# Local attention divides by its softmax sums behind the weighted sums of the values, not ahead of them

## What is computed

```python
x = x + local_block(group_norm(x))          # 4 groups of images, 8 strips of windows each
h = layer_norm(x) * g + b; h = roll(h, 3, 3)
h = windows of 7x7 pixels                    # 16 images * 64 windows, L = 49 tokens each
q, k, v = split(h @ qkv_w.T + qkv_b)         # 4 heads of 8 channels
scores = q @ k.T / sqrt(8) + bias
attn = exp(scores - max) / sum(exp(scores - max))   # softmax over the 49 keys
o = (attn @ v) @ out_w.T + out_b
y = gelu(layer_norm(o) @ mlp_w1.T + mlp_b1) @ mlp_w2.T + mlp_b2
```

## Time and profile before

| what | value |
|---|---|
| median of three executions | 3361.59 us |
| the profiled execution | 3363.74 us |
| its span, from first to last instruction | 3361.9 us |
| mean granted clock of TensorE in it | 0.951 of full speed |
| the local block's units, first subtraction to last product ahead of them | about 98 to 975 us of the span |
| PE, DVE, ACT, POOL busy, whole span | 88%, 74%, 65%, 18% |

### The profile page before, as it was taken

How to read it: one execution, slowest core, us unless ns; L and a number is a source line. 1 busy time by engine, 2 the same in 40 slices (tenths; PEclk the granted TensorE clock), 3 DMA queues, 4 the chain that set the end, 5 groups by cost and what they waited for, 6 DMA issues and landing times.

```text
span 3361.9 us, 66302 instructions
## 1 busy us (share of the span) xinstructions
PE 2950.1 (88%) x23401; PEld 1258.3 (37%) x23401; DVE 2471.9 (74%) x3210; ACT 2200.9 (65%) x3825; POOL 619.9 (18%) x497
## 2 busy tenths in 40 slices
PE   3788888888868999999999999999999999999775
PEld 2444444444435233333333333333333333333354
DVE  6788888888847877767777767777777777787342
ACT  2477776676755577767767767767777776777520
POOL 0444444444430101101101101001001011011100
PEclk7899999999989899999999999999999999999876
DMA  3000000000018010110110110101101101100022
GB/s 83 6 15 14 14 14 14 14 14 14 14 56 303 7 20 1 20 21 1 20 21 1 21 20 2 21 3 19 20 2 20 20 2 21 20 1 1 7 37 40
DMA packets 130451, 81.57 MB, mean 24 GB/s; under 512 B 111285, under 2 KB 120086, under 8 KB 129174
## 3 DMA queue, kind: packets, MB, share of 16 engines
q1 hardware_dynamic: 128629, 78.26, 9.5%
q10 hardware_dynamic: 1568, 0.04, 0.0%
HBM read 39.57 MB, written 32.11 MB: 21 GB/s over the span
## 4 chain that ended last, share of the span: by engine, by line
PE 59%; DVE 14%; issue 12%; POOL 6%; ACT 6%; DMA 2%; ACTq 1%; POOLq 0%; SPq 0%; DVEq 0%
PE ps L1531 18%; PE ps L1508 15%; PE ps L1478 14%; DVE arena L1117 7%; POOL arena L512 3%; PE ps L1541 2%; POOL arena L518 2%; ACT arena L667 1%; ACT L693 1%; PE ps L1358 1%; PE ps L1590 1%; PE ps L1490 1%; DMA arena<-in_x 1%; DVE arena L964 1%; POOL arena L528 1%
## 5 line engine op out<-in xcount | busy, mean ns | idle before, releaser
L1117 DVE TENSOR_REDUCE arena<-ps 128x2 f32<-128x896 f32 (+1 forms) x1408 | 1485.1, 1082 | 460.6 <-PE ps L1478 447.1
L800 ACT ACTIVATE arena<-ps 128x512 f32<-128x512 f32 (+1 forms) x2464 | 1377.4, 595 | 553.8 <-PE ps L1508 543.4
L1508 PE MATMUL ps<-arena 97*128 97x512 f16 (+1 forms) x2800 | 898.9, 360 | 24.6 <-issue 20.0
L1478 PE MATMUL ps<-arena 96*128 96x448 f16 x2800 | 775.9, 360 | 36.0 <-DVE arena L1117 27.1
L1531 PE MATMUL ps<-arena 128*32 128x512 f32 (+1 forms) x6176 | 685.4, 521 | 17.5 <-DVE arena L1139 17.0
L1508 PEld LDWEIGHTS ps<-arena 97*128 97x128 f16 (+1 forms) x2800 | 255.7, 100 | 708.0 <-ACT arena L800 462.5
L1478 PEld LDWEIGHTS ps<-arena 96*128 96x128 f16 x2800 | 256.8, 99 | 322.7 <-DVE arena L1117 108.3
L577 POOL TENSOR_TENSOR tok<-arena,tok 128x128 f32 (+3 forms) x112 | 47.9, 427 | 1585.4 <-DVE arena L1139 1585.4
L518 POOL TENSOR_TENSOR arena<-arena 113x784 f32<-113x784 f32 x128 | 192.4, 1503 | 428.9 <-DVE arena L967 428.9
L1531 PEld LDWEIGHTS ps<-arena 128*32 128x32 f32 x6176 | 131.5, 111 | 255.0 <-ACT arena L800 138.7
L512 POOL TENSOR_TENSOR arena<-arena 113x784 f32<-113x784 f32 x128 | 192.2, 1502 | 128.6 <-DVE arena L958 128.6
(11 more groups left out here) (180 smaller groups left out, 2787.5 us busy)
## 6 DMA issues: line engine op xcount, KB each, us to landing
arena<-qk_scratch SPq DMA_DIRECT2D x96, 196.0 KB, 4.1
qk_scratch<-arena SPq DMA_DIRECT2D x16, 448.0 KB, 4.9
arena<-ximg SPq DMA_DIRECT2D x16, 400.0 KB, 7.0
arena<-in_x SPq DMA_DIRECT2D x4, 1568.0 KB, 8.5
xa_scratch<-arena SPq DMA_DIRECT2D x32, 196.0 KB, 1.9
res_scratch<-arena SPq DMA_DIRECT2D x32, 196.0 KB, 2.1
arena<-xa_scratch SPq DMA_DIRECT2D x4, 1568.0 KB, 8.0
arena<-res_scratch SPq DMA_DIRECT2D x4, 1568.0 KB, 11.9
```

The lines of the kernel that those rows point to most:

```text
L800: act.activation(pk[0:rows, x % DEPTH, QC * m:QC * m + n], ps[0:rows, w % SB, 0:n], ACT.Exp, scale=float(C) ** -0.5).then_inc(att["exp"], 1)
L1117: dve.tensor_reduce(mxp[0:rows, p, 2 * u:2 * u + k], ps[0:rows, at_:at_ + k, 0:KN], AX_X, ALU.max)\
L1478: last = pe.matmul(ps[0:rows, MB + 2 * (j % 2) + n % 2, 0:KN], q2[p][0:96, T * t:T * t + rows], k2[p][0:96, KN * m:KN * m + KN], start=Tru ...
L1508: last = pe.matmul(ps[0:rows, bank, at_ % QC:at_ % QC + chunk_cols(c)], k2[p][0:97, T * t:T * t + rows], q2[p][0:97, QC * c:QC * c + chunk ...
```

## The change

The exponentials are no longer normalised before they are transposed. ScalarE writes them straight into `pr`, TensorE's transposes wait for them, and the value product uses them as they are. Behind the value product, eight more products per unit multiply the transposed exponentials (113 columns each) by the 0/1 columns `vhead` of the constants: their result holds, for each channel's partition and each query, the sum of the exponentials of its head. ScalarE copies value sums and sums together (211 columns) into a new buffer `avs`. VectorE takes reciprocals of the 113 columns in place (`reciprocal_sums`, in place of `sums`), and GpSimd multiplies the 98 columns by them into `oc` (`weight`, in place of `probabilities`). The weighted sums have one place in PSUM now, not two.

The order changes with it. On VectorE the reciprocals of a unit stand behind `values_copy` of two units later; those of a chunk's last unit open the next chunk, behind `bias_and_max(v+5)`. On GpSimd `weight(v)` stands behind `subtract(v+2)`. On TensorE `out_projection(n)` stands behind `values(v+1)`. New waits: exponentials for the transposes of two units earlier, the bias for exponentials of two units earlier, ScalarE's copy for the `oc` count of two units earlier, GpSimd's first `weight` of a chunk for the out-projection.

```diff
-            def probabilities(v, u):
+            def weight(v, u):
+
                 i = u % 2
                 pool.wait_ge(conv["rsum"], v + 1)
-                pool.tensor_tensor(pr[0:113, i, :].rearrange("p (m k) -> p m k", k=64)[:, :, 0:L],
-                                   ex[0:113, i, :].rearrange("p (m k) -> p m k", k=L),
-                                   mx[0:113, 2 + i, :].rearrange("p (m o) -> p m o", o=1)
-                                   .broadcast_to([113, GB * NH, L]), ALU.mult).then_inc(conv["prob"], 1)
+                pool.tensor_tensor(oc[:, :].rearrange("p (r w c) -> p w r c", r=WS, c=WS)[:, 2 * u:2 * u + 2],
+                                   avs[:, i, 0:2 * L].rearrange("p (w r c) -> p w r c", r=WS, c=WS),
+                                   avs[:, i, 2 * L:2 * L + 128].rearrange("p (w q) -> p w q", w=2)[:, :, 0:L]
+                                   .rearrange("p w (r c) -> p w r c", c=WS), ALU.mult).then_inc(conv["oc"], 1)
...
                     v = it * NU + u
-                    if u + 1 < NU or pre:
-                        probabilities(v + 1, u + 1)
                     if u == 0 and post:
                         residual(it - 2)
                     if u + 2 < NU or pre:
                         subtract(v + 2, u + 2)
+                    if u == 0 and not (isinstance(it, int) and it == 0):
+                        pool.wait_ge(ln[1]["center"], it)
+                    weight(v, u)
...
             def exponentials(v, u):
                 act.wait_ge(conv["sub"], v + 1)
-                act.activation(ex[0:113, u % 2, :], sc[0:113, u % 2, :], ACT.Exp).then_inc(conv["exp"], 1)
+                if not (isinstance(v, int) and v < 2):
+                    act.wait_ge(conv["ptrans"], v * 2 - 2)
+                act.activation(pr[0:113, u % 2, :].rearrange("p (m k) -> p m k", k=64)[:, :, 0:L],
+                               sc[0:113, u % 2, :].rearrange("p (m k) -> p m k", k=L), ACT.Exp).then_inc(conv["exp"], 1)
...
                 act.wait_ge(conv["av"], v + 1)
-                at_ = 4 * C * 2 + 2 * L * (u % 2)
-                act.activation(oc[:, :].rearrange("p (r w c) -> p w r c", r=WS, c=WS)[:, 2 * u:2 * u + 2],
-                               ps[:, VB_, at_:at_ + 2 * L].rearrange("p (w r c) -> p w r c", r=WS, c=WS), ACT.Copy)\
-                   .then_inc(conv["oc"], 1)
+                if not (isinstance(v, int) and v < 2):
+                    act.wait_ge(conv["oc"], v - 1)
+                act.activation(avs[:, u % 2, 0:2 * L + 113], ps[:, VB_, 2 * GB * C:2 * GB * C + 2 * L + 113], ACT.Copy)\
+                   .then_inc(conv["avc"], 1)
...
-            def sums(v, u):
-                i = u % 2
-                dve.wait_ge(conv["exp"], v + 1)
-                dve.tensor_reduce(mx[0:113, 2 + i, :], ex[0:113, i, :].rearrange("p (m k) -> p m k", k=L), AX_X, ALU.add)\
-                   .then_inc(conv["sum"], 1)
-                dve.wait_ge(conv["sum"], v + 1)
-                dve.reciprocal(mx[0:113, 2 + i, :], mx[0:113, 2 + i, :]).then_inc(conv["rsum"], 1)
+            def reciprocal_sums(v, u):
+
+                dve.wait_ge(conv["avc"], v + 1)
+                w = avs[:, u % 2, 2 * L:2 * L + 113]
+                dve.reciprocal(w, w).then_inc(conv["rsum"], 1)
...
                 v, n = it * NU, it - 1
+                if post:
+                    reciprocal_sums(v - 1, NU - 1)
                 values_copy(v + 1, 1)
...
                 probs_b(v, 0)
-                sums(v + 1, 1)
                 bias_and_max(v + 2, 2)
                 if post:
                     normalize(n, 1, XB, xn2[:, :])
                 values_copy(v + 2, 2)
+                reciprocal_sums(v, 0)
                 probs_b(v + 1, 1)
                 if pre:
                     normalize(it + 1, 0, YB, xn[:, 1 - p, :])
-                sums(v + 2, 2)
                 bias_and_max(v + 3, 3)
                 values_copy(v + 3, 3)
+                reciprocal_sums(v + 1, 1)
                 probs_b(v + 2, 2)
                 if pre:
                     keys(it + 1)
-                sums(v + 3, 3)
                 if pre:
                     bias_and_max(v + 4, 0)
                 if post:
                     skip_connection(n)
                 if pre:
                     values_copy(v + 4, 0)
+                reciprocal_sums(v + 2, 2)
                 probs_b(v + 3, 3)
                 if pre:
-                    sums(v + 4, 0)
                     bias_and_max(v + 5, 1)
...
+                for pair in range(2):
+                    for j in range(GB):
+                        q = 113 * (2 * j + pair)
+                        last = pe.matmul(ps[C * j:C * (j + 1), VB_, 2 * GB * C + 2 * L:2 * GB * C + 2 * L + 113],
+                                         cv("vhead", 113)[:, C * pair:C * pair + C], pt[0:113, i, q:q + 113],
+                                         start=(pair == 0), stop=(pair == 1), skip_group_check=True)
                 last.then_inc(conv["av"], 1)
...
                 v, n = it * NU, it - 1
+                values(v + 1, 1, p)
                 if post:
                     out_projection(n)
-                values(v + 1, 1, p)
                 transposes(v, 0)
```

More of the change, by code:

```diff
@@ L164, in conv_attention_moe @@
         sc = carve(2 * GB * NH * L).rearrange("p (i n) -> p i n", i=2)
-        ex = carve(2 * GB * NH * L).rearrange("p (i n) -> p i n", i=2)
         pr = carve(2 * GB * NH * 64).rearrange("p (i n) -> p i n", i=2)
-        mx = carve(4 * GB * NH).rearrange("p (i n) -> p i n", i=4)
+        mx = carve(2 * GB * NH).rearrange("p (i n) -> p i n", i=2)
+        avs = carve(2 * (2 * L + 128)).rearrange("p (i n) -> p i n", i=2)
         pt = carve(2 * 8 * 113).rearrange("p (i n) -> p i n", i=2)
@@ L240, in conv_attention_moe @@
         conv = {n: sem("conv_" + n) for n in (
-            "xg", "qk", "qz", "kz", "score", "vprod", "bias", "max", "sub", "exp", "sum", "rsum", "prob", "ptrans", "pcopy_a",
+            "xg", "qk", "qz", "kz", "score", "vprod", "bias", "max", "sub", "exp", "avc", "rsum", "ptrans", "pcopy_a",
             "pcopy_b", "vcopy", "av", "oc", "hid", "gelu", "y", "t1", "rt", "stored")}
@@ L538, in chunk @@
                         subtract(v + 2, u + 2)
+                    if u == 0 and not (isinstance(it, int) and it == 0):
+                        pool.wait_ge(ln[1]["center"], it)
+                    weight(v, u)
             subtract(0, 0)
-            probabilities(0, 0)
             subtract(1, 1)
@@ L952, in bias_and_max @@
                 dve.wait_ge(conv["score"], v + 1)
+                if not (isinstance(v, int) and v < 2):
+                    dve.wait_ge(conv["exp"], v - 1)
                 dve.tensor_tensor(sc[0:113, i, :].rearrange("p (b j n) -> p b j n", b=2, j=2),
@@ L1061, in _ @@
             values_copy(0, 0)
-            sums(0, 0)
             bias_and_max(1, 1)
@@ L1072, in _ @@
             chunk(G * NC - 1, 1, pre=False)
+            reciprocal_sums(G * NC * NU - 1, NU - 1)
             attention_norm(G * NC - 2)
@@ L1310, in values @@
                 if not (isinstance(v, int) and v < 2):
-                    pe.wait_ge(conv["oc"], v - 1)
+                    pe.wait_ge(conv["avc"], v - 1)
                 elif v == 1:
@@ L1322, in transposes @@
                 i = u % 2
-                pe.wait_ge(conv["prob"], v + 1)
+                pe.wait_ge(conv["exp"], v + 1)
                 for k in range(2):
@@ L1340, in weighted_values @@
                         for j in range(GB):
-                            w = 2 * (u % 2) + hf
                             s_ = 256 * hf + 64 * j + C * pair
                             q = 113 * (2 * j + pair) + 64 * hf
-                            last = pe.matmul(ps[C * j:C * (j + 1), VB_, 2 * GB * C + L * w:2 * GB * C + L * (w + 1)],
-                                             vs[0:113, i, s_:s_ + C], pt[0:113, i, q:q + L], start=(pair == 0),
-                                             stop=(pair == 1), skip_group_check=True)
+                            pe.matmul(ps[C * j:C * (j + 1), VB_, 2 * GB * C + L * hf:2 * GB * C + L * (hf + 1)],
+                                      vs[0:113, i, s_:s_ + C], pt[0:113, i, q:q + L], start=(pair == 0),
+                                      stop=(pair == 1), skip_group_check=True)
+                for pair in range(2):
[4 more added lines that the diff above has]
+                                         start=(pair == 0), stop=(pair == 1), skip_group_check=True)
                 last.then_inc(conv["av"], 1)
```

## The result

The changed kernel takes 3454.8 us (median of four, 3450.5 to 3457.6), the kernel before in the same comparison 3362.6 us: 1.0274 times as long, 95% interval 1.0256 to 1.0292. That is 92 us more, where 87 us were forecast, inside the range of 3398 to 3489 us.

The account below looks back on a forecast made before the run. A ring of waits through several engines sets the beat, TensorE close behind. Terms of +3.15, -1.07, +0.44, -0.37 give 29.6 us a chunk, +0.8 for the clock 30.4; over 31 passages +87 us: 3449 us, range 3398 to 3489.

Parts of the forecast that it names:

- W to O: From a chunk's last `weighted_values` (W) to the out-projection (O): 4.08 us, 3.15 us later than before.
- O to V: From the out-projection (O) to `values(v+3)` (V), TensorE's own run: 12.5 us, -1.07.
- V to K: From `values(v+3)` (V) to the small product behind the keys (K), reciprocals ahead of the keys: 5.20 us, +0.44.
- K to W: From the small product behind the keys (K) to the next chunk's last `weighted_values` (W): -0.37 us, gelus ending earlier.
- The clock: Falls of TensorE's granted clock with the longer wait ahead of the out-projection: +0.8 us a chunk, bounds 0.15 and 2.
- Rival 1: No more falls of TensorE's clock than before: 29.7 us a chunk, +67 us, 3429 us; chance 0.28.
- Start and end: Outside the 31 passages: start gains up to 2.8 us, end loses 1.6 us, together taken as zero.
- The faster case: Slack takes up the out-projection's delay: 27.1 us a chunk, -15 us, 3347 us; chance 0.08.
- the free point: Out-projection at W + 1.9 us, W being the chunk's last `weighted_values`: a delay up to there costs nothing.
- rival 4: Two clock falls a chunk behind the out-projection, multiplication near 1.0 us: +143 us, 3505 us, half 3475; chance 0.10.

Follow-up runs that it names:

- e1: Changed kernel with GpSimd's multiplication for a chunk's last unit placed ahead of the subtraction of the unit two later; 3402.4 us.
- e2: As e1, and on VectorE the reciprocals of a chunk's last unit between the bias and the maximum of the unit two later; 3372.3 us.
- e5: Changed kernel with two more 128x392 products on constants ahead of the out-projection's wait, their result overwritten; 3415.1 us.
- e4: Changed kernel with reciprocals of 16 of the 113 columns, the others multiplying by the sums themselves; 3451.1 us.
- e3: Changed kernel without the eight products a unit that form the sums, output not normalised; 3467.6 us.
- e8: As e5, without the eight products a unit that form the sums, output not normalised; 3412.7 us.

## Why the prediction was right

**W to O** was forecast at 4.08 us. It is 4.14 (520.32 to 524.46), by the chain named: scores, bias, maximum, subtraction, multiplication. The reciprocals (0.854 us, forecast 0.83; the estimate of 1.06 us that the prediction set beside it was too long) ended ahead of the subtraction, the multiplication took 0.379 us in the mean and 0.44 at this place (forecast 0.40). e1 and e2 took the chain apart and moved the out-projection to the points that the same sums gave, W + 3.38 and W + 2.83.

**O to V** was the term with two errors. At full clock it was forecast at 12.5 us and is 11.95 (e5). Half of that is the group of new products, which was mis-sized: 0.88 us for both groups from start to start against 0.49 for the old one is 0.39, where 0.52 was taken, twice. The rest, about 0.3 us, is the smaller gaps between products, which the prediction put at 0.3 us and which came to about 0.6: from the second `values` to its transposes, for one, 0.78 us before (516.11 to 516.89) and 0.58 in e5. With the clock it is 13.41 us.

**V to K** was forecast at 5.20 and is 5.15; **K to W** at 7.80 and is 7.88. That ScalarE's chain stands close behind the keys, so that cheaper reciprocals win next to nothing, is what e4 shows.

**The clock** was forecast at +0.8 us a chunk with bounds of 0.15 and 2, and is 1.47. The fall comes in almost every chunk, behind the wait at O: 24 of the 26 begin 0.1 to 1.4 us behind O, the other two at the keys. What it slows is the run that all others wait for. Size and frequency were both at the dear end. The two errors offset each other: 29.6 + 0.8 = 30.4 was forecast, 29.12 + 1.47 = 30.59 measured, so the sum came closer than its terms, and that 87 and 92 us lie so near each other is partly luck. Rival 1, no more falls than before, didn't come.

**Start and end** were taken as zero together. In the traces the first residual comes 1.1 us earlier (160.39 before, 159.26 after), the 31 passages take 96.0 us more, 3 more than the mean of the 27 gives, and what follows the block takes 1.0 us less: 93.9 us between the spans. So the start gained 1 us of the 2.8 allowed and the end lost 3 in place of 1.6, which is small either way.

**The rivals.** The faster case was to come if the out-projection stood by W + 1.9, and the prediction put it near W + 1.6 if GpSimd multiplied ahead of the subtraction. That was wrong: e1 does this and has it at W + 3.38, since the reciprocals behind the maximum then come last. With these moved too (e2) it is at W + 2.83, because the added products, the copy, the reciprocals and the multiplication still follow each other. By the prediction's sum, 0.9 us past the free point, e2 should lose 0.9 us a chunk; with the run from O to V 0.55 us shorter than forecast that leaves 0.35, or 11 us, as measured. An out-projection at W + 1.9 wasn't tried. In rival 4, 3475 us doesn't follow as the half of +143; nothing else was built on it.

## What to carry to other kernels

When a step moves to another place, walk the new order engine by engine and ask what stands ahead of it in each queue; here a multiplication of 0.4 us stood behind a subtraction that nobody needed yet. Of the 3.2 us by which the out-projection came later, that was 0.8, the reciprocals behind the maximum were another 0.55, and the new chain itself was the rest; still, with the clock, moving two instructions gave back 82 of 92 us. In this kernel a wait of TensorE of 2 us ahead of its longest run counted twice, once for itself and once for the clock behind it. And ask of a change what it unties, not only what it costs: with the sums off VectorE, a reorder that made the old kernel 2% slower made the new one faster than either.

## What the runs showed of the hardware

Less work on TensorE made the kernel slower, and more work faster: e3 leaves out 4 x 0.39 us of products a chunk and takes 13 us more, e5 adds 1.58 us and takes 40 us less. With a wait of 2.01 us at the out-projection the clock fell in nearly every chunk, and with 1.24 us (e1) in half of them. With 0.69 us (e2) it didn't fall there at all: the five falls of e2 begin 0.4 to 0.7 us behind the small product at the keys, where TensorE waits 1.33 us in all three kernels. The length of one wait doesn't decide it by itself: 1.73 us at the keys went with six falls in the kernel before and 1.72 us with 21 near the keys in e8. What made the difference stays open.

VectorE's group norm on 128x371 elements (L946 before, L950 after) took 1.25 us in the kernel before and 0.58 in the changed one, with the same instruction. In both it ended 0.23 us behind the end of the subtraction that ran on GpSimd: 512.88 against 512.65, and 524.24 against 524.01. Before:

```profile
511.15 1.50 POOL L512 TENSOR_TENSOR arena<-arena 113x784 f32<-113x784 f32 x1 [0.33 <-DVE arena L958]
...
511.63 1.25 DVE L946 TENSOR_SCALAR arena<-ximg,gn 128x371 f32 x1
```

After:

```profile
523.66 0.58 DVE L950 TENSOR_SCALAR arena<-ximg,gn 128x371 f32 x1
```

In e2, where the subtraction overlaps it again, it takes 1.31 us. In all twelve traces, in every chunk between 200 and 900 us, it ends 0.23 or 0.24 us behind the subtraction; in both traces above it takes 0.50 us at 82.47 us, ahead of the first subtraction. e4 is the nearest to a test, since its shorter reciprocals only let VectorE begin earlier under the subtraction: 1.14 us, and again the end is 0.23 us behind, 520.10 against 519.87.

```profile
518.37 1.50 POOL L512 TENSOR_TENSOR arena<-arena 113x784 f32<-113x784 f32 x1 [4.30 <-DVE arena L964]
518.96 1.14 DVE L950 TENSOR_SCALAR arena<-ximg,gn 128x371 f32 x1
```

So VectorE's instruction doesn't get done while GpSimd's runs, whenever it starts. The Trainium skill (GPSIMD Engine Reference, 1. Specifications) says that GpSimd's SBUF interfaces are shared with VectorE and contended by some of its instructions; the ends agree with that, though no run here took the subtraction away, and that the interface is the cause isn't shown.
